# Head attention: value products in two halves per unit, row maxima turned on VectorE and joined by 16 small transfers

## What is computed

```python
q = (src @ Wq).reshape(Bb, Tt, H, DH).transpose(0, 2, 1, 3)
k = (src @ Wk_c @ Wk).reshape(Bb, Tt, H, DH).transpose(0, 2, 1, 3)
v = (src @ Wv_c @ Wv).reshape(Bb, Tt, H, DH).transpose(0, 2, 1, 3)
...
attn = jnp.einsum('bhqd,bhkd->bhqk', q, k) / np.sqrt(DH).astype(np.float32)
attn = jax.nn.softmax(attn, axis=-1)
sa = jnp.einsum('bhqk,bhkd->bhqd', attn, v)
```

## Time and profile before

| | |
|---|---|
| median of 3 runs | 1607.37 us (1606.39 to 1608.2) |
| profiled execution, its own time | 1609.09 us |
| its span in the trace | 1607.4 us |
| busy over the span: TensorE matmul / VectorE / ScalarE / GpSimd | 1441.3 / 1183.3 / 835.2 / 368.6 us |
| TensorE clock granted, mean of the span | 0.964 |

### The profile page before, as it was taken

The page is one execution under the profiler, slowest core; times in us unless marked ns, Lnnn a source line. Parts: engine busy times, 40 slices in busy tenths (PEclk is TensorE's granted clock), DMA queues, the critical chain, the costliest instruction groups (busy, mean ns, idle before and its releaser), DMA issues. The chain is left out here.

```text
span 1607.4 us, 21813 instructions
## 1 busy us (share of the span) xinstructions
PE 1441.3 (90%) x7856; PEld 833.6 (52%) x7856; DVE 1183.3 (74%) x1733; ACT 835.2 (52%) x1507; POOL 368.6 (23%) x314
## 2 busy tenths in 40 slices
PE   7998799779999999999999998859999999999994
PEld 4665677423333333333233332348887888878873
DVE  3786766788888888888888888247677776876532
ACT  2454333128888888888888888812304214133130
POOL 0435802252310000000000000023235243262441
PEclk9999899759999999999999999979999999999997
DMA  5799765422444333333332230131141230411211
GB/s 193 273 320 345 248 175 138 81 69 62 102 70 60 60 60 61 61 54 61 61 56 51 48 68 21 39 113 55 39 106 20 87 86 21 106 28 53 54 14 13
DMA packets 105831, 145.89 MB, mean 91 GB/s; under 512 B 24048, under 2 KB 74624, under 8 KB 105728
## 3 DMA queue, kind: packets, MB, share of 16 engines
q1 hardware_dynamic: 84480, 107.13, 26.4%
q0 software_dynamic: 10784, 23.76, 6.7%
q10 hardware_dynamic: 10464, 13.64, 2.9%
HBM read 80.90 MB, written 63.06 MB: 90 GB/s over the span
## 5 line engine op out<-in xcount | busy, mean ns | idle before, releaser
L1532 DVE TENSOR_REDUCE i_saT<-h_sq 128x2 f32<-128x1024 f32 x512 | 601.0, 1218 | 75.4 <-PE h_sq L1416 75.4
L1498 ACT ACTIVATE h_p<-h_sk 128x512 f32<-128x512 f32 x999 | 543.4, 596 | 177.3 <-PE h_sk L1437 156.0
L1437 PE MATMUL h_sk<-h_q,h_k 50*128 50x512 f32 x999 | 252.0, 496 | 57.1 <-ACT h_p L1498 55.8
L1450 PE MATMUL h_po<-h_p,h_v 128*32 128x512 f32 x2048 | 276.2, 612 | 2.0 <-ACT h_o L1505 1.6
L1437 PEld LDWEIGHTS h_sk<-h_q,h_k 50*128 50x128 f32 x999 | 94.9, 185 | 340.1 <-ACT h_p L1498 327.4
L1416 PE MATMUL h_sq<-h_k,h_q 48*128 48x512 f32 x1024 | 195.8, 449 | 21.8 <-DVE i_saT L1532 14.4
L1755 PE MATMUL f_ob<-w_experts,f_h 128*128 x768 | 179.5, 393 | 0.0
L1755 PEld LDWEIGHTS f_ob<-w_experts,f_h 128*128 128x128 f32 x768 | 143.8, 188 | 31.6
L1668 POOL TENSOR_TENSOR f_h<-h_place,f_h 128x512 fp32r<-128x512 f32 x64 | 83.9, 1317 | 289.5 <-ACT f_h L1820 289.5
L1416 PEld LDWEIGHTS h_sq<-h_k,h_q 48*128 48x128 f32 x1024 | 101.0, 194 | 93.5 <-DVE i_saT L1532 77.1
L1816 ACT ACTIVATE f_x1p<-f_pair 128x1024 fp32r<-128x1024 f32 x8 | 8.2, 1026 | 226.1 <-PE f_pair L1068 226.1
(11 more groups left out here) (211 smaller groups left out, 1734.3 us busy)
## 6 DMA issues: line engine op xcount, KB each, us to landing
h_q<-q_d SPq DMA_DIRECT2D x84, 128.0 KB, 5.9
h_k<-k_d SPq DMA_DIRECT2D x84, 128.0 KB, 6.9
ot_d<-h_o ACTq DMA_DIRECT2D x32, 256.0 KB, 3.6
q_d<-t_parts SPq DMA_DIRECT2D x12, 512.0 KB, 5.0
k_d<-t_parts SPq DMA_DIRECT2D x12, 512.0 KB, 5.1
h_place<-xs_d SPq DMA_DIRECT2D x8, 530.0 KB, 4.2
p_xin<-in_L_attn_x SPq DMA_DIRECT2D x8, 512.0 KB, 5.0
xn_d<-p_xn SPq DMA_DIRECT2D x8, 512.0 KB, 5.0
```

The costliest lines, as they stand in the source:

```text
L1437: ins = nc.tensor.matmul(spread_banks[bank_at(f + g)], k6[r][at, p, j * P:(j + 1) * P], q6[r][at, p, c * CH:(c + 1) * CH], start=True, sto ...
L1450: ins = nc.tensor.matmul(po[h * VW:(h + 1) * VW, :], vh[n % RING][:, j, h, :], probs[u % PR][:, h, :], start=j == 0, stop=j == QT - 1)
L1498: nc.scalar.activation(probs[u % PR][:, h, :], spread_banks[bank_at(f)], ACT.Exp, scale=DH ** -0.5).then_inc(exp_done, 1)
L1532: nc.vector.tensor_reduce(halfmax[n % 2][:, m, :], sq[slot % 2][:, :, :], AX.X, ALU.max)\
```

## The change

Three things are changed, all in `head_attention`.

1. `mix` gets an argument `part`. TensorE's loop now runs twice per unit, each time `score`, one item, and the `mix` of one half of the queries (256 columns, `part` 0 or 1). For the last keys of an accumulation (j = 7), part 0 does nothing and part 1 does all 512 columns.
2. `negm` is no longer turned on TensorE. `turn` transposes it on VectorE in squares of 32x32 (`BLOCK`), so that query block b stands on partitions 32b to 32b+31; it is split there, right after `larger`, and `shift` sends it by 16 transfers (4 blocks, 2 sides, 2 parts) of 16x32 values where there were 4 of 16x128. With it go the identity matrix and the places in the `h_sq` rotation that the turned maxima had.
3. The first pass runs 5 units ahead (`LEAD`), and `take_out` and `store` come one fill earlier in ScalarE's order (`TAKE`).

```diff
+BLOCK = 32
+SQUARES = P // BLOCK
...
         PER = ITEMS // UNITS
+        PARTS = PAIRS
+        assert PER == PARTS
         BANKS = 3
-        LEAD = 4
-        HELD = PER
+        LEAD = 5
...
-        ident = room.take(P)
         halfmax = [room.take(ITEMS, SIDES) for i in range(2)]
         negm = room.take(TILES)
-        mparts = sb("h_mparts", [TILES, SHIFT, P], F32R)
+        assert TILES == BLOCK
+        turned = room.take(BLOCK)
+        mparts = sb("h_mparts", [P, SHIFT, BLOCK], F32R)
...
         def item_slot(n, m):
-            return n * ITEMS + m + max(0, n - 1 + (n >= 1 and m >= HELD))
-        def turn_slot(n):
-            return (n + 1) * ITEMS + n + (HELD if n + 1 < STEPS else 0)
+            return n * ITEMS + m
...
-        shifts_of = lambda n: (n // RING + 1) * SIDES * SHIFT * 16
+        shifts_of = lambda n: (n // RING + 1) * SIDES * SHIFT * SQUARES * 16
...
-                nc.gpsimd.memset(ident, 0.0).then_inc(const_set, 1)
-                pool.wait_ge(const_set, 1)
-                nc.gpsimd.affine_select(out=ident, in_=ident, compare_op=ALU.not_equal, fill=1.0,
-                                        base=0, pattern=[[-1, P]], channel_multiplier=1).then_inc(const_set, 1)
...
                 def shift(n):

-                    r, slot = n % RING, turn_slot(n)
-                    wait.ge(sq_free[slot % 2], slot // 2 + 1)
-                    for g in range(SIDES):
-                        for j in range(SHIFT):
-                            row = g * SIDE_AT + DOTS + j
-                            sp.dma_start(q6[r][row:row + 1, :, :].rearrange("o p t -> o (p t)").bitcast(F32),
-                                         mparts[g * PAIRS * QT:(g + 1) * PAIRS * QT, j, :].bitcast(F32))\
-                                .then_inc(shifted[r], 16)
+                    r = n % RING
+                    wait.ge(m_split, n + 1)
+                    for b in range(SQUARES):
+                        for g in range(SIDES):
+                            for j in range(SHIFT):
+                                row = g * SIDE_AT + DOTS + j
+                                at = b * BLOCK + g * PAIRS * QT
+                                queries = q6[r][row:row + 1, :, :].rearrange("o p (i b q) -> o (p i) b q", b=SQUARES, q=BLOCK)
+                                sp.dma_start(queries[:, :, b, :].bitcast(F32), mparts[at:at + PAIRS * QT, j, :].bitcast(F32))\
+                                    .then_inc(shifted[r], 16)
...
-                def turn_maxima(n):
-                    slot = turn_slot(n)
-                    pe.wait_ge(max_done, n + 1)
-                    pe.wait_ge(sq_free[slot % 2], slot // 2)
-                    nc.tensor.transpose(sq[slot % 2][0:TILES, 0, 0:P], negm, ident).then_inc(sq_made, 1)
...
-                def mix(n, w):
+                def mix(n, w, part):
                     c, j = divmod(w, QT)
-                    u = n * UNITS + w
-                    if j == 0:
-                        pe.wait_ge(out_taken, n * NQ + c)
-                    if w == 0 and n >= AHEAD:
-                        pe.wait_ge(spread, n - AHEAD + 1)
-                    pe.wait_ge(exp_done, (u + 1) * GH)
+                    u, last = n * UNITS + w, j == QT - 1
+                    if part == 0:
+                        if j == 0:
+                            pe.wait_ge(out_taken, n * NQ + c)
+                        if w == 0 and n >= AHEAD:
+                            pe.wait_ge(spread, n - AHEAD + 1)
+                        if last:
+                            return
+                    if part == 0 or last:
+                        pe.wait_ge(exp_done, (u + 1) * GH)
+                    at = slice(0, CH) if last else slice(part * CH // PARTS, (part + 1) * CH // PARTS)
                     for h in range(GH):
-                        ins = nc.tensor.matmul(po[h * VW:(h + 1) * VW, :], vh[n % RING][:, j, h, :],
-                                               probs[u % PR][:, h, :], start=j == 0, stop=j == QT - 1)
-                    ins.then_inc(pv_done, 1)
+                        ins = nc.tensor.matmul(po[h * VW:(h + 1) * VW, at], vh[n % RING][:, j, h, :],
+                                               probs[u % PR][:, h, at], start=j == 0 and part == 0, stop=last)
+                    if part == PARTS - 1:
+                        ins.then_inc(pv_done, 1)
...
-                for m in range(HELD):
-                    item(1, m)
-                pe.wait_ge(const_set, 2)
-                turn_maxima(0)
-                for m in range(HELD, LEAD * PER):
+                for m in range(LEAD * PER):
                     item(1, m)
                 for u in range(STEPS * UNITS + 1):
                     n, w = divmod(u, UNITS)
                     ahead = [divmod(u * PER + ITEMS + LEAD * PER + b, ITEMS) for b in range(PER)]
-                    if n < STEPS:
-                        score(n, w, 0)
-                    if ahead[0][1] == HELD and ahead[0][0] <= STEPS:
-                        turn_maxima(ahead[0][0] - 1)
-                    for coming in ahead:
+                    for part, coming in enumerate(ahead):
+                        if n < STEPS:
+                            score(n, w, part)
                         if coming[0] < STEPS:
                             item(*coming)
-                    if n < STEPS:
-                        score(n, w, 1)
-                    if u:
-                        mix(*divmod(u - 1, UNITS))
+                        if u:
+                            mix(*divmod(u - 1, UNITS), part)
...
-                TAKE = GH + 1
+                TAKE = GH
...
-                def round_maxima(n):
-                    slot = turn_slot(n)
-                    dve.wait_ge(sq_made, slot + 1)
+                def turn(n):
+                    dve.wait_ge(max_done, n + 1)
+                    nc.vector.transpose(turned, negm).then_inc(m_turned, 1)
+                    dve.wait_ge(m_turned, n + 1)
                     if n:
                         dve.wait_ge(shifted[(n - 1) % RING], shifts_of(n - 1))
-                    nc.vector.tensor_copy(mparts[:, HI, :], sq[slot % 2][0:TILES, 0, 0:P]).then_inc(m_rounded, 1)
-                def rest_of_maxima(n):
-                    slot = turn_slot(n)
+                    nc.vector.tensor_copy(mparts[:, HI, :], turned).then_inc(m_rounded, 1)
                     dve.wait_ge(m_rounded, n + 1)
-                    nc.vector.tensor_tensor(mparts[:, LO, :], sq[slot % 2][0:TILES, 0, 0:P],
-                                            mparts[:, HI, :].bitcast(F32), ALU.subtract)\
-                        .then_inc(sq_free[slot % 2], 1)
-                for n in range(STEPS + 1):
+                    nc.vector.tensor_tensor(mparts[:, LO, :], turned, mparts[:, HI, :].bitcast(F32),
+                                            ALU.subtract).then_inc(m_split, 1)
+                for n in range(STEPS):
                     for m in range(ITEMS):
-                        if n < STEPS:
-                            maximum(n, m)
-                        if n and m == HELD - 1:
-                            round_maxima(n - 1)
-                            rest_of_maxima(n - 1)
-                    if n < STEPS:
-                        larger(n)
+                        maximum(n, m)
+                    larger(n)
+                    turn(n)
```

3 lines of the change are left out of this document (2 added, 1 removed).

## The result

The changed kernel takes 1654.78 us (median of four runs, 1631.28 to 1679.18); the kernel before takes 1606.88 in the four runs beside them (1604.2 to 1608.2). The ratio of the times is 1.0215, with an interval of 1.0109 to 1.0321. Two runs of the changed kernel, those with the lowest mean clock (1679.18 and 1658.77 us), are left out of this ratio, and they include the profiled one; of the 44 runs of the kernel before that stand beside the runs of this document one (1842.18 us, at a mean clock of 0.829) is left out in the same way. The change makes the kernel slower: the interval lies above 1, and the fastest run after is 23 us above the slowest before. Whether it is slower by 2% the interval leaves open. The forecast was 1584.0, within 1574 to 1608.

A forecast was written before the change was run, and what follows sets the result against it. Bound: a loop of exponential latency to the second scores and a whole `mix` on PE back, 2.67 us a unit. Fifteen steps save 30, start and end add 3.4 and 3.3: -23.3 from 1609.09, median 1584, range 1574 to 1608.

The forecast's parts named there:

- The bound and the halves: Unit on PE: 1.25 us for the exponential's way plus 1.23 of PE work, 2.48 in all, 0.19 less than before.
- Scores to item: On PE, from scores behind a `mix` to the item: 0.34 us, a term of the 1.23 per half.
- item to `mix`: On PE, from item to the `mix` behind it: 0.32 us, bounds 0.23 and 0.43, from a similar pair of scores.
- rival 3: PE can't be fed: 24 instructions per half at 0.054 us each make the unit 2.60, total 1602; chance 0.16.
- The unit with a whole `mix`: At j = 7 `mix` stays whole behind the second scores: 0.43 us more, twice a step.
- that with the copy: Next `mix` (j = 0) waits for the copy out of `h_po`: 0.12 us more, twice a step.
- The chain of the maxima: From unit 10's first scores: split done at 4.2 us, first transfer 4.3, 16 transfers 0.61 apart, last landed at 15.4.
- The unit behind the split: VectorE's chain, 0.67 us longer, delays the next item's reduction by 1 us and holds PE up by about 0.2.
- The failed step: At each step's first scores PE waits about 0.5 us: transfers land at 15.4, six units end at 14.9.
- rival 4: Transfers become the bound: 0.1 us more spacing costs 22 us, gain gone from 0.71 apart, 1616 at 0.75; chance 0.14.
- The ends: Start 3.4 us later because of the transfers, and step 15 3.3 us longer from added changes of kind and exposed weights.

The follow-up runs named there:

- halves_only: The kernel before with the halves alone (maxima turned on TensorE, 4 transfers, 4 units ahead, `take_out` one fill earlier): 1584.53 us, ratio 0.9895.
- a_half_dma: The changed kernel, still 5 units ahead, with only the 8 transfers of the high parts of the maxima (scores use 49 rows): 1584.5 us, ratio 0.9851.
- a_lead6: The changed kernel with `LEAD = 6` instead of 5, same instructions and 16 transfers: 1590.92 us, ratio 0.9896 to the kernel before.
- a_lead5: The changed kernel itself, unaltered, run again: median 1656.22 us in six runs (1615.62 to 1667.82).
- halves_10dma: `halves_only` with six more transfers of the same kind in each shift, to rows nobody reads: 1642.94 us, ratio 1.0253 to the kernel before.
- mixed_lead6: The changed kernel with 6 units ahead and whole `mix` in steps 0 and 15, halves in steps 1 to 14: 1579.68 us, ratio 0.9824.

## Why the prediction was wrong

**The bound and the halves: right.** The forecast said 1.25 and 1.23 between scores and a unit of 2.48; the trace has 1.25, 1.24 and 2.49. Scores to item 0.34 was kept, item to `mix` is 0.33 (0.32 forecast). The changes between `mix` and other matmuls cost what the earlier trace rows showed, and the supply of instructions did not become a bound (rival 3). The Trainium skill, TensorEngine Tiling (Array Packing), Key Properties, says that changing the tiling mode drains the engine; the trace agrees, as each half pays for its changes of kind. The unit with a whole `mix` is 2.93, 0.45 longer (0.43 forecast), and that with the copy 2.56, 0.08 longer (0.12). `halves_only` shows the size of this part by itself: -22 us.

**The chain of the maxima: right in its parts.** In the step of the full clock, unit 10 starts at 760.28 and the split ends 4.26 later (4.2 forecast); SP starts 0.1 behind it, and the first scores follow at 776.01, 15.73 later (15.4 forecast). The unit behind the split takes 2.72, 0.24 longer (0.2 forecast). In the mean the transfers are 0.66 apart instead of 0.61 (16 take 10.0 to 11.2 us), and they land in 1.7 instead of 1.9. So the wait is about 1 us on average instead of 0.5. By the forecast's own price, 22 us for 0.1, and with 0.2 less for the landing, this makes 1584 + 12 - 3 = 1593: still faster than before.

**The failed step** is what that wait costs: "So PE stands still for about 0.5 us per step, and everything behind that wait with it." The wait was priced at its own length, in the sum and in rival 4 alike ("Each 0.1 us more from transfer to transfer is 1.5 us per step on PE, 22 us in all"). In the trace of the changed kernel a wait of 0.81 us or more at a step's start was followed by 3 to 51 us at 1.2 GHz, in which a unit takes 4.32. That cost 75 to 80 us in the profiled execution, five times the 15.9 us of the waits. That it is the wait is shown from both sides: without the wait (6 units ahead, or 8 transfers) the kernel takes 1591 and 1584.5, and with the wait added to `halves_only` it goes from 1584.5 to 1643. Rival 4 had the right sign and the right place, but by its own price the transfers would have to be 0.71 apart to take the gain away; at the measured 0.66 it gives a faster kernel.

The second idle piece was in the order shown ahead of the prediction: a unit in which one item is all that stands between first and second scores. I priced it as no PE work, which it is, and did not see that it lies right behind the wait. How much of the fall is due to it is not settled (see above).

**The ends.** The first scores start 1.8 later and the first exponential 2.0 (3.4 forecast). The way from the first transfer to the first scores is 11.24, about as forecast (11.05); but `larger` ends at 336.69 in this trace where it ended at 338.47 before, and that is the difference. Nothing here shows why. Step 0 takes 2.4 more, for which nothing was forecast; it has some 4 units at the low clock, of 4.3 each, where the kernel before has 2 or 3, of 4.1. Step 15 and what follows take 6.0 more instead of 3.3: the units there do cost 0.34 more, and some of them ran at the low clock.

In sum, the central value would have been near for a kernel without the wait: `halves_only` and `a_half_dma` both have 1584.5. That they meet 1584 so closely is in part luck: `a_lead6`, which has all 16 transfers and no wait, has 1590.9, and step 0, whose time at the low clock was not forecast, takes 43 to 60 us in the traces of these three kernels.

## What to carry to other kernels

A wait on TensorE in the middle of dense work must not be priced at its length alone: here 1 us, with another half microsecond of idle time close behind in most cases, cost 5 us on average, so a chain that is forecast to end 0.5 us too late should get a unit more of distance. Look at what stands behind a wait too, for a place where the engine has nothing to do, and fill it; one kernel here supports that this helps, and it saved time in any case. When a kernel's time scatters by more than its usual share, put the granted clock of each run beside its time first.

## What the runs showed of the hardware

- TensorE fell to 1.2 GHz after short idle pieces in nearly full work: in the changed kernel behind all eleven step starts with a wait of 0.81 us or more (ten of them with 0.51 behind), behind none of four with up to 0.68. No length divides the cases: in `a_lead5` one of 1.14 was let pass, and in `halves_10dma` the clock fell behind 0.56 and 0.76 and not behind 0.77. In `mixed_lead6` two pieces of 0.61 and 0.64 in one unit were followed by a fall. The Trainium skill, TensorE: Matmul & The Clock Gate, describes such oscillation from micro-idle times between groups of matmuls (A second HAM failure mode: psum-queue depth-cycling); the traces agree, and add that one or two such pieces a step were enough. The advice of the Trainium skill, TensorE: Matmul & The Clock Gate, Why this matters for your kernels, speaks only of longer idle gaps than the ones named here.
- TensorE stayed at the low level for up to 68.3 us (`a_lead5`, from 981.5), in which its only idle pieces were the 0.52 at the start and one of 0.33. What ends such a stretch was not found.
- The price of the low clock is not a factor of two for the whole: a unit of halves takes 4.32 instead of 2.48, one with a whole `mix` in each unit 4.14 instead of 2.67.
- A transpose of 128x32 values in squares on VectorE takes 0.21 us, and a quarter of the bytes makes a small transfer no quicker to issue: 16 with 16 pieces of 128 bytes took 10.0 to 11.2 us, 0.63 to 0.71 apart, 4 with pieces of 512 bytes took 2.41, 0.61 apart.
